# An expert FFN by blocks of four sequences: from one loop per expert to an unrolled program of blocks

## The reference

```python
h = jax.nn.gelu(jnp.einsum('bsh,bhi->bsi', input_tensor, Wi_b) + bi_b[:, None, :], approximate=False)
o = jnp.einsum('bsi,bih->bsh', h, Wo_b) + bo_b[:, None, :]
r = o + input_tensor
mu = jnp.mean(r, axis=-1, keepdims=True)
var = jnp.mean(jnp.square(r - mu), axis=-1, keepdims=True)
y = (r - mu) * jax.lax.rsqrt(var + LN_EPS)
return y * g_b[:, None, :] + be_b[:, None, :]
```

## Time and profile before

| | |
|---|---|
| median of three timed runs | 149.77 us (149.15 to 151.67) |
| profiled execution, first to last instruction (span) | 147.0 us |
| mean granted clock of TensorE, as a share | 0.975 |
| data moved | 25.03 MB in 17710 packets |

### The profile page before, as it was taken

One profiled execution on the slowest core, in us unless ns is written; L12 is line 12 of the kernel. 1 busy time (PEld: TensorE's weight loads), 2 busy tenths in 40 slices (PEclk: granted clock), 3 DMA queues, 4 the chain that ended last, 5 costly groups with the idle time before them and its releaser, 6 DMA issues.

```text
span 147.0 us, 3876 instructions
## 1 busy us (share of the span) xinstructions
PE 118.9 (81%) x949; PEld 116.1 (79%) x949; DVE 115.8 (79%) x181; ACT 76.2 (52%) x126; POOL 68.8 (47%) x57
## 2 busy tenths in 40 slices
PE   0296968998999999497999979993999399977800
PEld 0195968997999999496999979992999299977800
DVE  2493457178988998995999699969996999679880
ACT  3022966677089408547933990299129912970000
POOL 3006570217614962404492659255925593570220
PEclk9999999999999999999999999999999968999995
DMA  4979996999818210293947488756124612020021
GB/s 108 384 214 357 342 322 139 287 384 302 327 37 276 57 36 18 72 379 98 311 84 303 113 282 264 245 119 233 34 71 121 211 33 66 13 60 18 0 55 36
DMA packets 17710, 25.03 MB, mean 170 GB/s; under 512 B 1616, under 2 KB 14480, under 8 KB 17552
## 3 DMA queue, kind: packets, MB, share of 16 engines
q10 hardware_dynamic: 9824, 14.42, 30.3%
q1 hardware_dynamic: 7856, 10.26, 23.1%
HBM read 22.58 MB, written 2.10 MB: 168 GB/s over the span
## 4 chain that ended last, share of the span: by engine, by line
issue 50%; POOL 20%; DMA 12%; POOLq 7%; SPq 6%; DVE 2%; DVEq 0%; PE 0%
POOL wo_lo L344 14%; DMA x_in<-x_dram 6%; POOL xs L355 6%; DMA bo_bc<-L_cond_bo_dram 5%; SPq L214 5%; POOLq L224 3%; POOLq L355 1%; DMA idx_i<-itok_B_dram 1%; SPq L224 1%; POOL rstd L362 1%; POOLq L56 1%; SPq L181 0%; POOLq L373 0%; POOLq L383 0%; POOLq L372 0%
## 5 line engine op out<-in xcount | busy, mean ns | idle before, releaser
L344 POOL TENSOR_TENSOR wo_lo<-wo_in,wo_hi 128x1024 fp32r<-128x1024 f32 x15 | 43.7, 2932 | 22.7 <-ACT wo_hi L425 22.7
L696 PE MATMUL preact<-xT_hi,wi_hi 128*128 128x256 f32 x144 | 42.1, 292 | 11.6 <-DVE wi_lo L569 6.1
L436 ACT ACTIVATE h<-preact,biT 128x256 f32<-128x256 f32 x72 | 28.3, 484 | 41.3 <-DVE h_lo L596 29.2
L596 DVE TENSOR_TENSOR h_lo<-h,h_hi 128x512 fp32r<-128x512 f32 x36 | 47.4, 1357 | 0.6 <-ACT h_hi L444 0.6
L696 PE MATMUL preact<-xT_lo,wi_hi 128*128 128x256 f32 x144 | 41.5, 288 | 0.0
L696 PE MATMUL preact<-xT_hi,wi_lo 128*128 128x256 f32 x144 | 41.4, 288 | 0.0
L696 PEld LDWEIGHTS preact<-xT_hi,wi_hi 128*128 128x128 f32 x144 | 28.3, 196 | 13.0 <-issue 13.0
L696 PEld LDWEIGHTS preact<-xT_hi,wi_lo 128*128 128x128 f32 x144 | 28.4, 197 | 0.0
L696 PEld LDWEIGHTS preact<-xT_lo,wi_hi 128*128 128x128 f32 x144 | 28.3, 197 | 0.0
L713 PE MATMUL sums_ps<-wo_hi,h_hi 128*128 128x256 f32 x144 | 23.9, 288 | 1.7 <-DVE r L537 1.6
L362 POOL TENSOR_TENSOR rstd<-var_eps,minus_half 128x2 f32<-128x2 f32 x9 | 8.6, 953 | 34.7 <-DVE var_eps L550 34.7
(11 more groups left out here) (57 smaller groups left out, 74.9 us busy)
## 6 DMA issues: line engine op xcount, KB each, us to landing
wo_in<-L_cond_Wo_dram ACTq DMA_DIRECT2D x7, 1024.0 KB, 6.1
wi_in<-L_cond_Wi_dram ACTq DMA_DIRECT2D x5, 1024.0 KB, 5.2
wi_in<-L_cond_Wi_dram SPq DMA_DIRECT2D x3, 1024.0 KB, 9.4
x_in<-x_dram SPq DMA_DIRECT2D x36, 64.0 KB, 2.8
y_dram<-xs SPq DMA_DIRECT2D x32, 64.0 KB, 2.1
bo_bc<-L_cond_bo_dram SPq DMA_DIRECT2D x1, 1024.0 KB, 7.0
wo_in<-L_cond_Wo_dram SPq DMA_DIRECT2D x1, 1024.0 KB, 6.6
gamma_bc<-L_cond_gamma_dram ACTq DMA_DIRECT2D x3, 256.0 KB, 5.6
```

What stands on the lines that cost most here:

```text
L344: nc.gpsimd.tensor_tensor(wo_half(wo_lo, e, half), wo_half(wo_in, e, half), wo_half(wo_hi, e, half).bitcast(FP32), ALU.subtract).then_inc( ...
L436: nc.scalar.activation(h[:, c, :], preact_chunk(c), ACT.Gelu, bias=biT[:, bass.ds(e * IC + c, 1)]).then_inc(gelu_done, 1)
L596: nc.vector.tensor_tensor(piece(h_lo, i), piece(h, i), piece(h_hi, i).bitcast(FP32), ALU.subtract).then_inc(h_lo_done, 1)
L696: last = nc.tensor.matmul(preact_chunk(c), w[:, e % 2, k, c * P:(c + 1) * P], xT[:, k, :], start=(k == 0 and w is wi_hi and xT is xT_hi), ...
```

## The change

The whole program is written anew. What it computes is the same, and it still makes 9 blocks, 96 matmuls of 256 columns for each. What differs:

- **Layout in DRAM.** The arrays are passed in other layouts: x also with tokens along the free axis (`x_columns`), each weight with one contiguous 8 KB row per partition, and bias, gamma, beta and the first bias in one array `vectors` (3,104 bytes for each of 128 partitions, per expert). TensorE's transposes of x are gone. x has 24 more sequences (zeros) for the slots of blocks that are not full; their results are stored too.
- **Per block, not per expert.** Each block loads both of its weights, its vectors, x by columns (`xT_in`, four DMAs) and x by rows (`xs`, four DMAs), and splits both weights. Expert 2's weights are loaded and split twice.
- **Unrolled.** There is no loop. A branch is taken only for a block beyond the eighth.
- **Who does what.** VectorE takes the low parts of the first weight (two pieces of 1024), of h (from PSUM, `preact`), of x (from SBUF), and of chunks 0 to 3 of the second weight (`wo_low(t, 0)`). GpSimd takes the low part of chunks 4 to 7 (128x4x256), x plus bias (two of 128x256) and one root per tile. ScalarE applies gelu in place in PSUM and makes the high parts in pieces of 1024.
- **The queues.** All loads and stores behind block 0's first ones are issued by SP. Each sequence's address is a table entry of its own, read just before its DMA.
- **Order.** TensorE alternates a quarter of block t's first product with a quarter of block t-1's second. The first weight and x of block t+1 are split on ScalarE and VectorE in the middle of block t.

The core of the diff:

```diff
-        def load_block(eng, t, tiles=(0, 1)):
-
-            words = {tile: word(eng, t, tile) for tile in tiles}
-            samples = samples_of(eng, words)
...
+        def sample(eng, t, j):
+            return entry(eng, QUAD * t + j, ROWS - 1)
...
+        def load_wi(eng, t, e):
+            if t >= 2:
+
+                eng.wait_ge(wi_lo_done, wi_count(t - 2, len(wi_pieces(t - 2)) - 1))
+            eng.dma_start(wi_in[:, t % 2, :, :, :].rearrange("p c k n -> p (c k n)"),
+                          wi[bass.ds(e, 1), :, :].rearrange("o p f -> (o p) f")).then_inc(wi_loaded[t % 2], 16)
...
+        def load_xT(eng, t, slots=range(QUAD)):
+            if t >= 2:
+                eng.wait_ge(x_ready, t - 1)
+            for j in slots:
+                b = sample(eng, t, j)
+                eng.dma_start(xT_in[:, t % 2, j, :, :].rearrange("p k s -> p (k s)"),
+                              xt[bass.ds(b, 1), :, :].rearrange("o p f -> (o p) f")).then_inc(xT_loaded[t % 2], 16)
...
+        def store(eng, t, tile):
+            eng.wait_ge(y_ready, 2 * t + tile + 1)
+            for j in (2 * tile, 2 * tile + 1):
+                b = sample(eng, t, j)
+                eng.dma_start(out[bass.ds(b, 1), :, :].rearrange("o s h -> (o s) h"), slot(t, j)).then_inc(
+                    stored[t % X_RING], 16)
...
+            load_xT(sp, 0, (0, 1))
+            second = expert(sp, 1)
+            load_wi(sp, 1, second)
+            load_xT(sp, 1)
+            load_params(sp, 1, second)
+            load_x(sp, 0)
+            load_wo(sp, 1, second)
+            load_x(sp, 1)
+            n = entry(sp, T_BLOCKS, MAX_BLOCKS, MIN_BLOCKS)
+
+            def iteration(t, ahead):
+                if ahead:
+                    e = expert(sp, t + 2)
+                    load_xT(sp, t + 2)
+                    load_wi(sp, t + 2, e)
+                    load_params(sp, t + 2, e)
+                    load_x(sp, t + 2)
+                if t >= 2:
+                    store(sp, t - 2, 1)
+                if ahead:
+                    load_wo(sp, t + 2, e)
+                if t >= 1:
+                    store(sp, t - 1, 0)
...
+            def iteration(t, has_next):
+                gelu(t, 0)
+                if has_next:
+                    wi_high(t + 1, 0)
+                h_high(t, 0)
+                gelu(t, 1)
+                if has_next:
+                    wi_high(t + 1, 1)
+                h_high(t, 1)
+                gelu(t, 2)
+                wo_high(t, 0)
+                h_high(t, 2)
+                gelu(t, 3)
+                wo_high(t, 1)
+                h_high(t, 3)
...
+            def iteration(t, has_next, has=True):
+                if t >= 1:
+                    h_low(t - 1, 3)
+                if t >= 2:
+                    centre(t - 2, 1)
+                if has:
+                    h_low(t, 0)
+                if t >= 2:
+                    finish(t - 2, 1)
+                if has_next:
+                    wi_low(t + 1, 0)
+                if has:
+                    h_low(t, 1)
+                if t >= 1:
+                    centre(t - 1, 0)
+                if has_next:
+                    wi_low(t + 1, 1)
+                if has:
+                    h_low(t, 2)
+                if t >= 1:
+                    finish(t - 1, 0)
+                if has_next:
+                    split_x(t + 1)
+                if has:
+                    wo_low(t, 0)
```

More of the change, by code:

```diff
@@ L28, with expert_ffn @@
 LN_EPS = 1e-12
[L31 to L35, removed]
+RAW_BANKS = ()
+def expert_ffn(nc, xr, xt, idx, wi, wo, par, out):
+    B = idx.shape[0]
+    S, H = xr.shape[1:]
+    E = wi.shape[0]
+    IC = wo.shape[2] // H
+    HC = H // P
+    QUAD = 4
     N = QUAD * S
-    HC, IC = H // P, I // P
+    MIN_BLOCKS = B // QUAD
     MAX_BLOCKS = (B + (QUAD - 1) * E) // QUAD
[L39 to L53, removed]
+    SLOTS = QUAD * MAX_BLOCKS
+    ROWS = B + SLOTS
+    BANKS = IC // 2
+    SPLIT = [q for q in range(BANKS) if q not in RAW_BANKS]
+    NS = len(SPLIT)
+    SPLIT_CHUNKS = 2 * NS
+    assert SPLIT == list(range(NS)) and NS >= 2
+    WO_PIECES = [(0, IC // 2), (IC // 2, SPLIT_CHUNKS)]
+    WARM_UP = 28
+    WO_RING, PAR_RING, X_RING = 3, 5, 6
+    T_EXPERT, T_BLOCKS = SLOTS, SLOTS + MAX_BLOCKS
+    T_ALL = T_BLOCKS + 1
     ctx = ExitStack()
@@ L99, in expert_ffn @@
+        idx_i = sb("idx_i", [B, B + 1], I32)
+        one_up = sb("one_up", [B, B + 1])
+        key = sb("key", [B, B + 1])
+        same = sb("same", [B, B])
+        after = sb("after", [B, B])
         before = sb("before", [B, B])
         ones = sb("ones", [B, B])
[L101 to L106, removed]
@@ L123, in sums @@
[L123 to L136, removed]
-        idx_loaded = sem("idx_loaded")
-        bi_loaded = sem("bi_loaded")
-        bo_loaded = sem("bo_loaded")
@@ L233, in sample @@
[L233 to L261, removed]
-            with eng.Else():
-                store_those_there(eng, n, samples, lambda tile, half: words[tile] // THERE[half] % 2)
@@ L265, in store_last_tile, with wi_pieces @@
-        def store_last_tile(eng, blocks, tile):
-            w = word(eng, blocks, tile, 1)
-            samples = samples_of(eng, {tile: w})
-            there = [eng.snap(w // THERE[half] % 2) for half in range(TILE)]
-            eng.wait_ge(y_ready, blocks * 2 + (2 * STORE_LAG - 3 + tile))
-            store_those_there(eng, blocks, samples, lambda tile, half: there[half])
+        def wi_pieces(t):
+            n = 4 if t == 0 else 2
+            return [(i * IC // n, (i + 1) * IC // n) for i in range(n)]
@@ new lines, in wi_count, with wi_count_of_chunk, flat, loads_of @@
+        def wi_count(t, piece):
+            return piece + 1 if t == 0 else 4 + 2 * (t - 1) + piece + 1
+        def wi_count_of_chunk(t, c):
+            return wi_count(t, next(i for i, (a, b) in enumerate(wi_pieces(t)) if a <= c < b))
+        def flat(tile, t, chunks):
+            return tile[:, t % 2, chunks[0]:chunks[1], :, :].rearrange("p c k n -> p (c k n)")
+        def loads_of(t, ring):
+            return 16 * (t // ring + 1)
+        def entry(eng, at, hi, lo=0):
+            return eng.value_load(table[0:1, at:at + 1], min_val=lo, max_val=hi)
@@ L348, in add_bo @@
-            def add_bo(t):
-                e = expert(pool, word(pool, t, 0))
-                if is_first(t):
-                    pool.wait_ge(first_x_loaded, 16 * QUAD)
-                else:
-                    pool.wait_ge(x_loaded, t * (16 * QUAD))
-                for tile in range(2):
-                    nc.gpsimd.tensor_tensor(xs_rows(t + 1, tile), x_tile(t, tile),
-                                            bo_bc[:, bass.ds(e, 1), :].rearrange("p o h -> p (o h)"),
-                                            ALU.add).then_inc(x_biased, 1)
@@ L392, in _, with residual @@
-            root(blocks)
+                                    pattern=[[-1, B]], channel_multiplier=1).then_inc(const_step, 1)
+            def residual(t):
+                pool.wait_ge(x_loaded[t % X_RING], 4 * loads_of(t, X_RING))
+                pool.wait_ge(par_loaded[t % PAR_RING], loads_of(t, PAR_RING))
+                for tile in range(2):
+                    nc.gpsimd.tensor_tensor(xs[:, t % X_RING, tile, :], xs[:, t % X_RING, tile, :], row(0, t),
+                                            ALU.add).then_inc(xs_ready, 1)
@@ new lines, in iteration, with end @@
+            def iteration(t, has):
+                if t >= 1:
+                    wo_low(t - 1)
+                if t >= 2:
+                    root(t - 2, 1)
+                if has:
+                    residual(t)
+                if t >= 1:
+                    root(t - 1, 0)
+            def end(t):
+                iteration(t, False)
+                root(t - 1, 1)
+            pool.wait_ge(table_ready, 1)
+            n = entry(pool, T_BLOCKS, MAX_BLOCKS, MIN_BLOCKS)
+            for t in range(MIN_BLOCKS):
+                iteration(t, True)
@@ L482, in _, with wi_high @@
-            blocks = all_blocks(act)
-            store_last_tile(act, blocks, 1)
+            load_xT(act, 0, (2, 3))
+            load_wo(act, 0, e)
+            n = entry(act, T_BLOCKS, MAX_BLOCKS, MIN_BLOCKS)
+            def wi_high(t, piece):
+                a, b = wi_pieces(t)[piece]
+                if t == 0:
+                    act.wait_ge(first_wi_loaded[a // (IC // 2)], 16)
+                else:
+                    act.wait_ge(wi_loaded[t % 2], loads_of(t, 2) - (16 if t % 2 == 0 else 0))
+                if t >= 2:
+                    act.wait_ge(preact_ready, BANKS * (t - 2) + BANKS)
+                nc.scalar.activation(flat(wi_hi, t, (a, b)), flat(wi_in, t, (a, b)), ACT.Copy).then_inc(wi_hi_done, 1)
@@ L485, in _, with end @@
+            def end(t):
+                act.nop()
+            for piece in range(4):
+                wi_high(0, piece)
+            for t in range(MIN_BLOCKS - 1):
+                iteration(t, True)
```

(36 more changed lines are left out.)

745 lines of the change are left out of this document (293 added, 452 removed).

## The result

The changed kernel takes 174.0 us in the median (173.28 to 178.66, 4 runs), the one before 149.69 in the same session: a ratio of 1.161, 95% interval 1.155 to 1.167. Forecast were 185 us, in a range from 165 to 201, and a slower kernel with a chance of 0.86. One of the four runs (178.66) is over 1.5% above the fastest and is left out of the ratio, as is one of `e7` (144.98). The profiled execution took 174.23 us and spans 172.5, with a mean granted clock of 0.906.

What follows compares the result with a forecast made beforehand. SP's issuing was taken as the bound, 18.7 us a block: block 8's turn at 132.5, its first weight landing at 144.6, x ready 155.4, end 182.8, plus 2.8 around the span: 185.6, rounded 185; range 165 to 201.

Steps and rivals of the forecast that it cites:

- 80 x 1.34: SP's 80 small DMAs before block 8's loads, each with read, address and issue at 1.34 us: 107.2 us.
- Its lower end: On SP, reads that hide behind the issue ahead take 0.3 us off each of 80: -24, giving 161; range from 165.
- The 2.8: Time around the kernel's span, taken as before: 2.8 us added to 182.8.
- SP without waits: Sign on SP's queue: small DMAs 1.3 us apart for the whole run with hardly a wait.
- Starts of blocks on TensorE are 18 to 19 us apart: Sign on TensorE that SP is the bound, at 18.7 us a block.
- TensorE's busy share falls below 70%: Sign on TensorE that SP is the bound, beside its clock falling several times.
- blocks under 15 us and VectorE without gaps: Two signs, in block spacing and on VectorE, that would show the forecast of SP as the bound wrong.
- GpSimd's hold: GpSimd's one piece holds two-input work for up to 2.3 us a block; taken as 0.5.
- the first rival: SP not the bound, a sequence costing under 0.9 us; VectorE then bounds, at 148 or 143 us; chance 0.14.
- much of what stands there reads PSUM: Reason given for taking 0.5 us, not 2.3, for work that GpSimd's piece holds up in a block.
- the term of 2 us: Added to TensorE's last products because its clock falls to 0.5 after idle time and then comes back: 2 us.
- The third rival: TensorE's clock falls in each block's idle time and stays down: 18.6 us a block, about 210 in all; chance 0.03.

Runs made afterwards that it cites:

- e7: As e6, with SP loading block 2's columns and first weight ahead of the rows of blocks 0 and 1: 142.3 us, 0.951 of the kernel before.
- e1: The changed kernel with SP reading each sequence's table entry once and keeping the register: 159.1 us, 1.069 of the kernel before.
- e2: The changed kernel with SP reading every sequence's table entry twice in a row: 224.0 us in one run.
- e3: The changed kernel with the same bytes of x in 3 issues instead of 8 for each block but the first: 157.0 us, 1.051 of the kernel before.
- e6: As e1, with one wait added so that GpSimd starts its half only after VectorE's half: 145.3 us, 0.969 of the kernel before.
- e5: As e1, with GpSimd's half of the second weight's low part moved to VectorE: 147.4 us, 0.984 of the kernel before.

## Why the prediction was right

**The mechanism** was the one forecast: a table read ahead of each small DMA makes SP the bound, the first weight behind four of them comes late, and engines that work in order pass the delay on. `e1`, `e2` and `e3` show it from three sides.

**The sum by its terms.** The first read after the table is ready began at 6.0 (forecast 6.2). SP came to block 8 at 122.5, not 132.5. This is the term that was mis-sized: "80 x 1.34". The 30 sequences by columns took 1.10 each, the 32 by rows about 1.24 and the 18 stores about 1.26, together 95.4 instead of 107.2. Two parts of the sequence were dearer in the row it was taken from: the address operation was 0.11, because the kernel before unpacks it from a word, and is 0.04 for a plain entry; and the issue of a load by columns is 0.33, not 0.50. The range had an end for dearer issues of 128 rows and none for cheaper ones. Its lower end stood for reads that hide behind the issue ahead of them, and `e2` shows that none hides; that 174 lies well inside is in this part luck. The single entries and weights, and issues that stretched, cost about 2 us more than forecast. From there: first weight's landing 132.7 (144.6 forecast; 4.8 instead of 5.9 after the issue), x ready 11.4 us later (10.8), TensorE's last matmul 20.7 us after that (19.6), the end 7.7 later (7.8), and 1.7 instead of 2.8 around the span. The errors are -10.0, -1.9 (0.8 of it before the issue), +0.6, +1.1, -0.1 and -1.1: together -11.4, from 185.6 to the 174.2 of the profiled execution. The 2.8 was a median less the span of one faster execution; where the time and the span are of the same execution they lie 1.7 us apart (148.77 and 147.1 for the kernel before, beside `e1`).

**SP without waits** was right up to its last load. Other signs came out differently. "Starts of blocks on TensorE are 18 to 19 us apart": they are 14.2 to 14.4 in the middle, where the engines worked off the lead that SP's short turns had given them, then 19.1, 17.6 and 17.1. "TensorE's busy share falls below 70%": it is 72. And two of the signs that were to show the forecast wrong, blocks under 15 us and VectorE without gaps, did stand between 60 and 93 us, though the forecast cause held: they say which engine is slowest in a stretch, not which queue sets the end.

**GpSimd's hold** was taken as 0.5 us a block. In the changed kernel it is 2.1 or 2.2 in seven of the nine blocks: three times on `wo_low(t, 0)`, between 60 and 93 us, once on the cast, and three times on `finish`, as here:

```profile
105.82 2.57 DVE L514 SCALAR_TENSOR_TENSOR xs<-centred,rstd,params 128x256 f32<-128x256 f32 x1
```

The forecast time holds this term once, behind the last landing, where it was 2.1 instead of 0.5; the other parts of that stretch came out 1.0 us shorter. In the blocks before, SP hid it. It was wrong for the first rival: with SP relieved the kernel takes 159, not the 143 to 148 worked out there. The step that failed is "much of what stands there reads PSUM". In `e1` the program's order puts VectorE's half and GpSimd's half at the same moment, each released by ScalarE's high parts, and both read SBUF.

**TensorE's clock** fell in idle stretches and came back, as the term of 2 us assumed. The third rival did not come.

**Two readings** of the prediction are off without effect. A block moves 3.3 MB, not 3.1 (29.83 MB in nine blocks), so 18.7 us a block would be 177 GB/s, still under the 226 of the earlier trace rows. And at half clock matmuls start 0.21 us apart, not 0.19.

**Reads and the shared port.** 115 reads on SP have a median of 268 ns. With the operations behind it a read costs 0.55, which `e2` shows as added time. The floor of about 600 ns for a register load that the Trainium skill gives (DMA: Bandwidth & Descriptors, "Latency and other measured facts") does not hold here. VectorE's half takes 3.40 us beside GpSimd's and 1.22 without it, and `e6` gets the difference back by order alone. The Trainium skill (SBUF — State Buffer, section "SBUF: two separate sides") says that VectorE with two SBUF inputs and a GpSimd operation that reads SBUF share a port pair, and that the one that starts first keeps it for its whole instruction; the rows of `e1` agree, where GpSimd starts 0.1 us ahead. They bear out the order and not the exact length: `centred` in `e6` ends 0.28 us after GpSimd's half, less than its own 0.48.

## What to carry to other kernels

An engine that only issues DMAs never looks busy in a page. Count what its queue has to do for one turn of the loop, including the register loads ahead of each address, and compare that with the turn. Read an index once and keep the register. Put the large load that everything waits for ahead of the small ones: `e7` shows this for the start alone (3.0 us), and within a block's turn it wasn't tried. Where two engines hold each other up, the order of their work can be worth at least as much as its division (145.3 us in `e6`, 147.4 in `e5`): make the streaming operation of one begin where the other has work from PSUM.

## What the runs showed of the hardware

- The issue on SP has two prices here, in the median: 0.33 us for the loads by columns, the first weight and the vectors, and 0.48 for the loads by rows and stores of 64 rows; single ones took up to 1.64. The loads by rows fell to 0.33 when they were made two sequences (128 rows) at a time in `e3`:

```profile
L215 SPq DMA_DIRECT2D xs<-x_rows x18: 333/333/493, 13.0 to 103.7; - x18
```

 But the second weight's load, with 128 rows as the first's, takes 0.49 in the median of the changed kernel (0.45 to 1.21), and the loads by rows, unchanged, took 0.55 in `e1`. What decides is open; it wasn't tried.
- In the changed kernel the granted clock was 0.5 (1.2 GHz) for 3.4 or 6.8 us at five places before the end. Each time it fell inside one of TensorE's five longest idle stretches since its first product, of 4.1 to 8.1 us, and came back while TensorE worked. Matmuls of 256 columns then start 0.21 us apart instead of 0.12.
- A VectorE cast from SBUF to SBUF is held by GpSimd as a two-input operation is: 2.56 against 0.42 us, seen once.
